# Attention 1 written out, its mask on VectorE, the join spread over its neighbours, and the keys' rotary ahead of the queries'

## The reference

```
x = x + layernorm(attention1(layernorm(x)))
x = x + layernorm(ffn(layernorm(x)))

attention1: 16 heads of 16, q,k,v = x @ W.T, scores * 16**-0.5, causal mask,
            softmax, @ v, @ Wo.T
ffn(z):     h = rmsnorm(z, ln1_w)
            q = rope(h @ Wq) (32 heads of 128); k = rope(h @ Wk), v = h @ Wv (4 heads of 128)
            scores / sqrt(128), causal mask, softmax, @ v, @ Wo;   z1 = z + that
            t = rmsnorm(z1, ln2_w); sigmoid router over 32 experts, top 8 by score + bias
            z1 + sum of experts silu(t@Wg)*(t@Wu)@Wd by gate + a shared expert
```

## Time and profile before

| what | value |
|---|---|
| median of 3 runs | 960.92 us (959.73 to 962.18) |
| profiled execution | 961.15 us, of which the traced span is 959.1 us |
| PE busy | 870.1 us (91%) |
| DVE busy | 624.5 us (65%) |
| ACT busy | 569.9 us (59%) |
| POOL busy | 456.0 us (48%) |
| mean granted TensorE clock | 0.969 of full speed |
| stages by the trace | prepare to 25.4, attention 1 to 183, join to 213.4 (first scores of attention 2), attention 2 to about 620, experts to the end |

### The profile page before, as it was taken

One profiled execution on the slowest core, in us unless ns is written; L12 is line 12 of the kernel. 1 busy time (PEld: TensorE's weight loads), 2 busy tenths in 40 slices (PEclk: granted clock), 3 DMA queues, 4 the chain that ended last, 5 costly groups with the idle time before them and its releaser, 6 DMA issues. The chain is left out here.

```text
span 959.1 us, 18782 instructions
## 1 busy us (share of the span) xinstructions
PE 870.1 (91%) x6108; PEld 804.9 (84%) x6108; DVE 624.5 (65%) x1620; ACT 569.9 (59%) x1572; POOL 456.0 (48%) x480
## 2 busy tenths in 40 slices
PE   4699999467999999999999999978999999999994
PEld 2589899456999998999899999967888888888884
DVE  7366666656788788877778777765545444444546
ACT  4788888455776766667666676654443334333333
POOL 5633334156766776777766777720222222221221
PEclk9999999778999999999999999997999999999998
DMA  6000100311114111141111111200433333333321
GB/s 210 23 1 24 44 23 1 99 34 38 41 46 134 44 44 35 44 134 45 33 46 40 40 46 45 51 1 17 142 116 110 99 114 103 110 115 115 104 88 44
DMA packets 50246, 63.34 MB, mean 66 GB/s; under 512 B 5728, under 2 KB 36064, under 8 KB 50176
## 3 DMA queue, kind: packets, MB, share of 16 engines
q1 hardware_dynamic: 49088, 61.41, 21.9%
q10 hardware_dynamic: 1088, 1.05, 0.3%
HBM read 41.86 MB, written 1.18 MB: 45 GB/s over the span
## 5 line engine op out<-in xcount | busy, mean ns | idle before, releaser
L637 POOL TENSOR_TENSOR b_prob<-b_prob,b_rsum 128x256 f32<-128x256 f32 (+1 forms) x128 | 104.9, 840 | 111.0 <-DVE b_rsum L619 111.0
L73 PE MATMUL banks<-act_t,b_w 128*128 128x256 f32 (+1 forms) x392 | 130.1, 332 | 1.9 <-DVE moe_hid L1994 1.0
L75 PE MATMUL banks<-act_t,b_w 128*128 128x256 f32 (+1 forms) x392 | 128.0, 327 | 0.0
L74 PE MATMUL banks<-act_t,b_w 128*128 128x256 f32 (+1 forms) x392 | 127.9, 326 | 0.0
L1898 ACT ACTIVATE moe_hid<-banks 128x512 fp32r<-128x512 f32 x66 | 39.5, 598 | 124.2 <-DVE banks L1989 124.2
L1298 ACT ACTIVATE b_prob<-banks,b_negmax 128x128 f32<-128x128 f32 (+1 forms) x256 | 103.6, 417 | 14.1 <-DVE b_negmax L1285 14.0
L1982 DVE TENSOR_TENSOR moe_gated<-banks,moe_share 128x512 f32<-128x512 f32 x66 | 45.6, 691 | 85.4 <-PE banks L75 81.8
L1156 ACT ACTIVATE b_qt<-b_work 128x512 fp32r<-128x512 f32 x64 | 40.4, 632 | 90.0 <-POOL b_work L1151 90.0
L1151 POOL TENSOR_TENSOR b_work<-b_work 128x512 f32<-128x512 f32 x64 | 86.6, 1353 | 9.5 <-DVE b_work L1139 0.4
L637 POOL TENSOR_TENSOR a_prob<-a_prob,a_rsum 128x256 f32<-128x256 f32 x64 | 51.6, 828 | 81.4 <-DVE a_rsum L619 81.4
L1147 POOL TENSOR_TENSOR b_work<-b_work,rope_t 128x512 f32<-128x512 f32 x64 | 83.2, 1300 | 7.9 <-DMA b_work<-b_work 7.9
(11 more groups left out here) (229 smaller groups left out, 3041.4 us busy)
## 6 DMA issues: line engine op xcount, KB each, us to landing
b_work<-b_work SPq DMA_DIRECT2D x128, 128.0 KB, 2.3
moe_share<-gates SPq DMA_DIRECT2D x32, 512.0 KB, 3.6
b_w_raw<-in_b_wq SPq DMA_DIRECT2D x4, 1024.0 KB, 5.4
b_w_raw<-in_b_wo SPq DMA_DIRECT2D x4, 1024.0 KB, 9.1
a_src_t<-act_t SPq DMA_DIRECT2D x5, 512.0 KB, 2.9
moe_w_raw<-in_wg SPq DMA_DIRECT2D x16, 128.0 KB, 2.2
moe_w_raw<-in_wu SPq DMA_DIRECT2D x16, 128.0 KB, 2.3
moe_w_raw<-in_wd SPq DMA_DIRECT2D x16, 128.0 KB, 2.2
```

Source lines behind the costliest of these rows:

```text
L73: nc.tensor.matmul(out, w_lo, m_hi, start=start, stop=False, skip_group_check=skip)
L74: nc.tensor.matmul(out, w_hi, m_lo, start=False, stop=False, skip_group_check=skip)
L75: return nc.tensor.matmul(out, w_hi, m_hi, start=False, stop=stop, skip_group_check=skip)
L637: last = self.m.nc.gpsimd.tensor_tensor(rows, rows, rsum[:, :, t:t + 1].to_broadcast([PART, 2, width]), ALU.mult)
```

## The change

The constants lose the two bf16 masks; `prepare` clears 2048 and 1024 columns where it cleared 9216 and 4096, and the cleared columns that attention 1 still needs (4096 and 2048) are now POOL's first work inside attention 1, ahead of the memset of `acc`; ACT waits for them (`zeroed`) before the first values and the second query stack. Attention 1 is written out, reads the activations in place, and SP copies nothing. Its mask matmuls go; DVE's reduction becomes the one of attention 2 (mask added, minimum taken) and the sign moves into the weights' scale and the exponential. Half of the join (batches 0 and 1, and the statistics of batch 2) moves into the last two iterations and the drain of attention 1, the other half into the first slots of attention 2, whose keys and queries of batch 0 are now PE's first work there. In attention 2 `pool_kv` stands ahead of `pool_rotate`.

```diff
@@ prepare, POOL
-            nc.gpsimd.memset(m.b_w[:, 2 * B_W:4 * B_W].bitcast(F32), 0.0)
-            nc.gpsimd.memset(m.q_stack[:].bitcast(F32), 0.0)
+            nc.gpsimd.memset(m.q_stack[:, 0:NTT * HPI * PART].bitcast(F32), 0.0)
+            k_at = 2 * B_W + 2 * NTT * HPI * PART
+            nc.gpsimd.memset(m.b_w[:, k_at:k_at + NTT * HPI * STACK].bitcast(F32), 0.0)
@@ attention 1, PE scores
-            nc.tensor.matmul(self.diagonals(h), m.ident16[:], self.mask_twice(), start=True, stop=False,
-                             skip_group_check=True)
@@ attention 1, DVE maximum
-                last = nc.vector.tensor_reduce(self.negmax[:, p % 2, t, h:h + 1],
-                                               m.s_ps[:, h, lo:lo + width], AX, ALU.max, negate=True)
+                row = m.s_ps[:, h, lo:lo + width]
+                last = nc.vector.tensor_tensor_reduce(
+                    row, row, m.mask_neg[:, SEQ - width:SEQ], 1.0, -NEG, ALU.add, ALU.min,
+                    accum_out=self.negmax[:, p % 2, t, h:h + 1])
@@ attention 1, POOL ahead of the acc memset
+            nc.gpsimd.memset(self.v.rearrange("p a t h n -> p (a t h n)").bitcast(F32), 0.0).then_inc(self.zeroed, 1)
+            nc.gpsimd.memset(m.q_stack[:, NTT * HPI * PART:].bitcast(F32), 0.0).then_inc(self.zeroed, 1)
@@ attention 1, what stands behind slot k (0 is the first slot of the drain): POOL, PE, ACT, DVE
+                if k == -5:
+                    pool.wait_ge(self.qt_full, PAIRS * (self.ITS - 1))
+                    join.pool_attention(pool, 0)
+                if k == -4:
+                    join.pool_attention(pool, 1)
+                if k in (2, 3):
+                    join.gpsimd(pool, k - 2)
...
+                if k in (3, 4):
+                    if k == 3:
+                        pe.wait_ge(self.exp_done, 2 * PAIRS * self.ITS)
+                    join.turn.tensor(pe, k - 3)
...
+                if k == -6:
+                    m.norm_a.roots(act, 0)
+                    m.norm_a.roots(act, 1)
+                if k == 0:
+                    join.norm_f.roots(act, 0)
+                    join.norm_f.roots(act, 1)
+                    m.norm_a.roots(act, 2)
+                if k in (1, 2):
+                    join.act_input(act, k - 1)
+                if k in (3, 4):
+                    join.turn.scalar(act, k - 3)
...
+                if k in (-8, -7, -2):
+                    b = {-8: 0, -7: 1, -2: 2}[k]
+                    m.norm_a.moments(dve, b, lambda t: acc[:, t, :], arrived)
+                if k == -6:
+                    m.norm_a.factors(dve, 0)
+                    m.norm_a.factors(dve, 1)
+                if k in (-4, -3):
+                    join.dve_add(dve, k + 4)
@@ attention 2, slot_pool
             self.pool_normalise(pool, (P - 1) % PAIRS, P - 1)
+        if it + 1 < self.ITS and p in self.ROPE_AT:
+            self.pool_kv(pool, it + 1, self.ROPE_AT[p])
         if self.runs(P + 2):
             self.pool_rotate(pool, P + 2)
-        if it + 1 < self.ITS and p in self.ROPE_AT:
-            self.pool_kv(pool, it + 1, self.ROPE_AT[p])
@@ attention 2, PE ahead of its slots
-            turn.tensor(pe, 0)
-            pe.wait_ge(turn.lo_done, 1)
             self.pe_kv(pe, 0, self.KV0)
-            turn.tensor(pe, 1)
             self.pe_kv(pe, 0, self.KV1)
             self.pe_queries(pe, 0)
-            turn.tensor(pe, 2)
             self.pe_queries(pe, 1)
-            turn.tensor(pe, 3)
             self.pe_kv(pe, 0, self.KT)
             self.pe_queries(pe, 2)
-            pe.wait_ge(turn.lo_done, NB)
```

More of the change, by code:

```diff
@@ L675, in slot_dve, with run @@
             self.dve_values(dve, it)
-        if p == 0 and not (isinstance(it, int) and it < 2):
+        if p == 0 and it >= 2:
             self.dve_add(dve, it - 2)
-    def run(self, eng, slot, middles, after=None):
-        for it in range(2):
-            for p in range(PAIRS):
-                slot(eng, it, p)
-        for first, last in middles:
-            self.splitting = last <= self.ITS - NB
-            with eng.Fori(first // self.UNROLL, last // self.UNROLL) as step:
-                for k in range(self.UNROLL):
-                    self.parity = k
-                    for p in range(PAIRS):
-                        slot(eng, step * self.UNROLL + k, p)
-        for it in range(middles[-1][1], self.ITS):
+    def run(self, eng, slot, after=None):
+        for it in range(self.ITS):
             for p in range(PAIRS):
                 slot(eng, it, p, units=it < self.ITS - 1)
+                if after:
+                    after(PAIRS * (it - self.ITS) + p)
         for k in range(self.DRAIN):
@@ L989, in _, with after @@
             split_weights(3)
-            self.run(act, self.slot_act, middles)
-            for b in range(NB - 1):
-                m.norm_a.roots(act, b)
+            def after(k):
+                if k == -6:
[9 more added lines that the diff above has]
+                    join.turn.scalar(act, k - 3)
+            self.run(act, self.slot_act, after)
         @block.vector
@@ L1182, in pe_kv @@
         wait(pe, self.w_ready, 4 * (it // NB) + 3)
+        if it < NB:
+            wait(pe, self.join.turn.lo_done, it + 1)
         if u == self.KV0:
@@ L1309, in pe_values @@
         wait(pe, self.o_ready, P)
+        if P == 0:
+            wait(pe, self.join.turn.lo_done, 3)
         pt = lambda part: self.prob_t[:, p % 2, part, :]
@@ L1320, in pe_project @@
         wait(pe, self.o_ready, P + 1)
+        if P == 0:
+            wait(pe, self.join.turn.lo_done, NB)
         if p == 0:
@@ L1474, in slots @@
             slot(eng, P)
-            for stage, b in plan.get(P - self.STAGES, ()):
+            for stage, b in plan.get(P - self.STAGES, ()) + plan.get(("first", P), ()):
                 stage(b)
@@ new lines, in tiles, with pool_attention @@
+    def tiles(self, b):
+        return range(NTT * b, NTT * (b + 1))
+    def pool_attention(self, pool, b):
+        pool.wait_ge(self.norm_a.ready, b + 1)
+        for t in self.tiles(b):
+            last = self.m.nc.gpsimd.tensor_scalar(self.rows[:, t, :], self.acc[:, t, :],
+                                                  self.norm_a.factor[:, 0, t:t + 1],
+                                                  self.norm_a.shift[:, 0, t:t + 1], ALU.mult, ALU.add)
+        last.then_inc(self.attn_ready, 1)
@@ new lines, in act_attention, with dve_add @@
+    def act_attention(self, act, b):
+        for t in self.tiles(b):
+            last = self.norm_a.apply(act, self.rows[:, t, :], self.acc[:, t, :], t)
+        last.then_inc(self.attn_ready, 1)
+    def dve_add(self, dve, b):
+        x, rows = self.m.x, slice(NTT * b, NTT * (b + 1))
+        dve.wait_ge(self.attn_ready, b + 1)
+        self.m.nc.vector.tensor_tensor(x[:, rows, :], x[:, rows, :], self.rows[:, rows, :],
+                                       ALU.add).then_inc(self.x1_ready, 1)
+        self.norm_f.moments(dve, b, lambda t: x[:, t, :], lambda t: dve.wait_ge(self.x1_ready, b + 1))
@@ L1675, in gpsimd, with act_input @@
+    def act_input(self, act, b):
+        for t in self.tiles(b):
+            last = self.norm_f.apply(act, self.rows[:, t, :], self.m.x[:, t, :], t, 1)
+        last.then_inc(self.turn.rows_ready, 1)
     def gpsimd(self, pool, b):
```

240 lines of the change are left out of this document (86 added, 154 removed).

## The result

The changed kernel took 973.11 us in the median of 4 runs (970.48 to 979.21), the kernel before 961.27 us beside them; the ratio, taken over all the runs and not from the two medians, is 1.0134 with a 95% interval of 1.0084 to 1.0184. The forecast of 979 us lies 6 us above that median. The profiled execution of the changed kernel is the slowest of its four, 979.21 us with a span of 977.4; the mean granted clock was 0.956 in it and 0.962 to 0.967 in the other three. So its trace probably holds some microseconds of low clock that the median has not; only the profiled execution has a trace, so this rests on the mean clocks.

What follows compares the result with a forecast made beforehand. PE was taken as the bound, busy 870.1 of 959.1 us, with ACT close in attention 1. From 961.15 us, -18 without the reorder, +24 for the reorder and +12 for the clock gave 979 us, range 943 to 989.

Steps and rivals of the forecast that it cites:

- dip in prepare's wake: Clock line of the kernel before: read as three dips, one in prepare's wake and two around the join.
- likeliest case: Whole kernel: join's gain arrives, the reorder costs 24 us and the clock 12, giving 979 us; chance 0.42.
- the rival on the other side: Attention 2: the reorder is hidden by slack, the clock stays and the rest comes through, 943 us; chance 0.24.
- the terms without the reorder: Prepare, attention 1, join and attention 2's start: -6.3 + 2 - 2.7 + 6.9 + 1.3 - 17.9 - 1.3 = -18.0 us.
- the reorder with its clock: Steady attention 2: keys' rotary ahead of the queries' costs +24 us, low clock behind PE's longer waits +12.
- The ring: Steady attention 2: POOL-ACT-DVE-POOL round of 6.1 us without slack; the keys add 1.05 us in two slots of four.
- One sign of the forecast: Profile after: the clock line would show eights and sevens in attention 2.
- the two readings on DVE beside the moved memsets: Start of attention 1: DVE held up to 4 us more beside POOL's memsets, or by the skill's rule not at all.
- The -2.7 for the mask: Steady attention 1: 64 mask matmuls go, 0.25 us an iteration for seven and 0.9 in the last; writing out costs nothing.
- The +6.9: Join's work inside attention 1: 3.0 us for ACT's table loads and roots, 3.9 for DVE's moments and additions.
- I come to 12.4 us: Attention 2, block start to first scores: 12.4 us instead of 30.3, -17.9, with PE in the lead for 9 us.
- "-1.3" for iteration 0: Attention 2, iteration 0: PE's wait for the key rows shrinks but transposes come in, -1.3 us, bounds -4 and +3.

Runs made afterwards that it cites:

- e1: Changed kernel with the queries' rotary put back ahead of the next keys' in attention 2: 948.38 us, ratio 0.9865 to the kernel before.
- e2: Kernel before with only the keys' rotary put ahead of the queries' in attention 2: 992.49 us, ratio 1.0334.
- e3: Changed kernel with 16 unneeded matmuls ahead of PE's wait for the keys at attention 2's iteration starts: 969.23 us, ratio 1.0074 to the kernel before.
- e7: Changed kernel with only the first half of the next keys rotated ahead of the queries, the second behind: 956.84 us, ratio 0.9933 to the kernel before.
- e8: Changed kernel with only the second half of the next keys rotated ahead of the queries, the first behind: 969.01 us, ratio 1.0066 to the kernel before.
- e6: Changed kernel with the queries rotated first and attention 1's masks back on PE, still written out: 950.32 us, ratio 0.9872 to the kernel before.
- e4: e1 with copies in place of the square roots of batches 0 and 1, so without two table loads: 944.99 us, ratio 0.9813 to the kernel before.
- e10: Changed kernel, queries first except in attention 2's iteration 0, plus 10 and 12 unneeded matmuls in PE's two waits before its first scores: 947.63 us, ratio 0.9855.

## Why the prediction was right

**What bounds.** The order of the views held: the windows pointed to the join and to attention 2, and the timeline of one iteration gave the step that decided. One reading of the clock line was wrong: it has no dip in prepare's wake. Its low digits are three slices around the join, from 168 to 240 us, one behind attention 2, from about 647 to 671, and the last; nothing in the sum hung on it. The forecast had its likeliest case right, and the rival on the other side, 943 us, turned out to be the time of the change without the reorder, within 6 us (e1).

**The number, in part luck.** 979 us is the profiled execution's 979.21 almost exactly, but by two misses that cancel: the terms without the reorder came to -11.5 us where -18 was forecast, counting the 1.7 us of the rest, and the reorder with its clock came to +29.8 where 36 was forecast. Each is off by 6 us and more. The direction and the mechanism are not luck: e1, e2 and e3 show them one by one.

**The reorder.** The ring was where the prediction put it, and e1, e2, e7 and e8 show it from four sides. The waits cost 22.3 us where 24 was taken. Alone, the first half costs 0.6 us an iteration of its 1.05 (e7), the second half all of it (e8, 14.8 in 14). An iteration takes 28.6 us where about 29 was forecast, and PE's wait came to 2.1 us in the mean, not 2.7 to 3.0.

**The clock.** It fell after six of 14 waits, taken were eight, and a stretch lengthened its slot by 1.5 us, as taken. Net of what the following slots gave back, it was 7.6 us in the profiled execution (e3) where 12 was taken. The other three runs had a higher mean clock, and this is probably most of the 6 us by which the median lies under the forecast; they left no trace to show it. One sign of the forecast did not come: the clock line has nines in all of attention 2 but its first slices, since 3.4 us at half clock lower the mean of a slice of 24 us by less than a tenth.

**Prepare, attention 1, the drain.** All within 1 us. Two slips in the working changed nothing: 6,144 columns at acc's rate take 5.4 us, not 5.3, and half of DVE's 7.6 us is 3.8, not 3.9. Of the two readings on DVE beside the moved memsets the one without a hold was right. The -2.7 for the mask is right in sum and not in its parts: writing attention 1 out, costed at nothing, gave about 1.2 us of the 2.9 (0.17 an iteration), and the mask gave the other part; in e6 this gain did not reach the kernel's time. The +6.9 came out at 6.5, and e4's trace bears its parts out: 2.9 us for the loads with the clock behind them where 3.0 was taken without it, 4.0 for the rest where 3.9 was.

**The join, mis-sized.** The step "I come to 12.4 us" measured 16.2, inside its bounds. It took PE to be in the lead; PE waited 2.52 us for the cosine products of the queries and 3.31 us for the first split. e10 shows that its low clock was not the reason. "-1.3" for iteration 0 measured +1.5, inside its bounds too: PE still waits 2.08 us for the key rows, behind the rotaries and the join's rows on POOL, and its clock was half for a while.

## What to carry to other kernels

An instruction that runs in an engine's idle time costs nothing only where it stands; moved ahead of something that another engine waits for, it costs up to its full length each round, as far as the round has no slack, even when a reader of it can start sooner. Before moving one, follow who ends the idle time on both sides of it. And where PE waits, price the wait twice: here a wait of 2.2 to 2.8 us cost, in six cases of nine, 1.5 us more in the slot behind it, at half clock. Unneeded matmuls in the wait gave that part back in steady attention 2, where PE is the bound, and nothing at the block's start, where it is not.

## What the runs showed that was not expected

The low clock mostly comes after the wait is over, and not every time: the same wait of 2.76 us was followed by half clock at 340.44 and by full clock at 455.97.

```profile
455.97 0.30 PE L73 MATMUL banks<-b_kt,b_qt 128*128 128x128 f32 x1 [2.76 <-DVE b_kt L1226]
455.90:461.00 5.10, 5.03 (x40) 4.91 (x41) 4.20 (x14) 3.44 (x13) 2.90 (x4) 1.00 0.22 51
```

In steady attention 2 it fell inside a wait once, in e8: at 252.2, 0.4 us before the end of the wait of 2.69 us. Where it falls may be what sets executions of one kernel apart, 970 to 979 us at mean clocks of 0.967 and 0.956; with one trace this is not shown.

POOL's sine product took 2.41 us instead of 1.30 in two of the steady iterations. Timeline of POOL and DVE in the changed kernel:

```profile
332.69 2.41 POOL L1160 TENSOR_TENSOR b_work<-b_work,rope_t 128x512 f32<-128x512 f32 x1
332.54 1.41 DVE L1357 TENSOR_TENSOR b_w<-b_w_raw,b_w 128x1152 fp32r<-128x1152 f32 x1
```

DVE's split of the next weights, which reads two operands of SBUF, had started 0.15 us earlier, and POOL's instruction took 1.1 us longer than it otherwise does. The Trainium skill (SBUF — State Buffer, Who interferes with whom) has this as a rule for such a pair, whichever comes first holding the other; the trace agrees, with POOL the one that is held. At 284.05 DVE is: the same split takes 2.43 us there, and POOL's sum L1164 had started 0.11 us earlier. The kernel before has such cases too, there with the rotary's sum L1151 held (2.27 us at 337.50): moving an instruction on POOL moves it against DVE's list too.
